# A selective-scan loop: the last 256 positions of a product moved to DMA and GpSimd, the other 768 formed one step ahead

## The chip, the cores and the metric

The kernel runs on one NeuronCore of a Trainium2 chip. The metric is the device time of one launch in microseconds. Below, PE is TensorE, DVE is VectorE, ACT is ScalarE, POOL is GpSimd, and SP is SyncE, which here issues the transfers.

## What is computed

Six residual layers on an image batch of 4 x 16 x 16 positions with 192 channels. The change touches the first alone, a state-space layer: after a projection, a 3x3 convolution and SiLU, four directions k are scanned over each image's 256 positions, for 96 channels with 16 states each, in float32:

```
def step(h, inp):
    u_t, d_t, B_t, C_t = inp
    dA = jnp.exp(d_t[..., None] * As)
    h = h * dA + (d_t * u_t)[..., None] * B_t[:, :, None, :]
    y = jnp.einsum('bkcn,bkn->bkc', h, C_t)
    return (h, y)
```

d is a softplus of a projection of the input; B and C are projections of it; u is the convolved input. The four directions are the image by rows, by columns, and both reversed. Their outputs are summed, normalised, gated by SiLU(z) and projected back to 192 channels. The other five layers (neighbourhood attention, a quantised transformer block, two expert layers and an attention) follow one after the other.

## The kernel before

All work is written out for each engine by hand, with semaphores between engines. The first layer is the function scan_layer. The 4 images of 256 positions lie side by side, so a row has T = 1024 columns. The 96 channels are cut into NG = 12 groups of 8, and a step puts 8 channels times 16 states on the 128 partitions. There are N = 48 steps (4 directions by 12 groups).

Ahead of the loop, ACT and DVE form d (tile dd) and d*u (tile du) for each direction on 96 partitions, and PE and ACT form B and C on 128 partitions (Bb, Cb). SP stores d in memory (scan_d, L438) and fetches it back for each step with each channel repeated for its 16 states (d_sp, L447), into NSP = 4 buffers.

Step n of the loop has these parts, each on its engine:

- ACT (L601): dA(n) = exp(A * d_sp) into PSUM banks 0-1 or 2-3. It waits until the scan of step n-2 has read that place.
- PE, spread(n) (L654): two matmuls with a 0/1 matrix (sel) copy the 8 rows of d*u to 128 partitions, in PSUM banks 4 and 5. Each half waits until the product of step n-1 has read it. A float32 matmul is recorded as two pieces.
- DVE (L502): two products dBu = (spread d*u) * Bb of 512 columns each, into one of two buffers.
- DVE (L509): the scan h = h * dA + dBu over 1024 columns into hs, one of two buffers. The sign of the step makes the reversed directions. It waits for both products of its step, for dA and for the product hC of step n-2.
- POOL (L470): hC = hs * Cb over 1024 columns, one of two buffers. For the last step DVE does it (L516).
- PE, add(n) (L669): two matmuls with selT sum the states of each channel and add the result in PSUM banks 6 and 7, which hold the sum y over steps.

PE's order is fixed by its own program, and each step n issues spread(n) and then add(n-2):

```
for n in range(N + 2):
    if n < N:
        spread(n)
    ...
    if n >= 2:
        add(n - 2)
```

Between spread(0) and spread(1) stands direct() (L659), two matmuls that need the last part of Cb. After the loop DVE, PE and ACT sum the directions, normalise, gate and project (L520 to L545).

Beside this, ACT quantises five weights for a later layer in some of the steps (L585), from a buffer that SP fills (L461).

Of the kernel before, what the change touches and what calls it, by code (L numbers as in the profile page):

```python
# [14 lines left out]
F32 = mybir.dt.float32  # L15
# [5 lines left out]
ALU = mybir.AluOpType  # L21
# [6 lines left out]
L = HW * HW  # L28
T = NB * L
C = 192  # L30
P = 128
CH = C // 2
NT = T // P
BANK = 512
NHALF = T // BANK
# [59 lines left out]
class GroupNorm:  # L95


    N = 2 * NB

# [97 lines left out]
DI = C // 2  # L197
NS = 16
RK = C // 16
CG = P // NS  # L200
NG = DI // CG
KD = 4
# [5 lines left out]
ORDER = (0, 2, 1, 3)  # L208
NSP = 4
# [4 lines left out]
def scan_layer(nc, const, X, D):  # L214
# [3 lines left out]
    with ExitStack() as stack:  # L218
        ctx = Ctx(nc, stack)
# [11 lines left out]
        sel = ctx.sb("sel", [DI, NG, P])  # L231
# [6 lines left out]
        zb = ctx.sb("zb", [DI, T])  # L238
        ps = ctx.ps("ps_l1", [P, 8, BANK])
        d_dram = nc.dram_tensor("scan_d", (KD, DI, T), F32, kind="Internal").ap()  # L240
        S = lambda n: ctx.sem(f"l1_{n}")
        loaded_xT = [S(f"loaded_xT{h}") for h in range(2)]
        loaded_g, loaded_w, loaded_p, loaded_s = S("loaded_g"), S("loaded_w"), S("loaded_p"), S("loaded_s")
# [6 lines left out]
        ordered, raw, bc_ps, bc_sb = S("ordered"), S("raw"), S("bc_ps"), S("bc_sb")  # L250
        soft_act, soft_vec, logged, d_ready, du_ready, A_done = (
            S("soft_act"), S("soft_vec"), S("logged"), S("d_ready"), S("du_ready"), S("A_done"))
        stored = [S(f"stored{k}") for k in range(KD)]
        spread_d = [S(f"spread_d{j}") for j in range(NSP)]
        started, dA_done, du_bc, dBu_done, scanned, weighted, y_added, y_out, weighted_last = (
            S("started"), S("dA_done"), S("du_bc"), S("dBu_done"), S("scanned"), S("weighted"), S("y_added"), S("y_out"),
            S("weighted_last"))
# [2 lines left out]
            S("turned"), S("stats"), S("var"), S("std"), S("rstd"), S("normed"), S("back"), S("gate"), S("res_ps"), S("res"))  # L260
        STEPS = 2 * NG
        N = 2 * STEPS
        banks = lambda a, b, rows=P: ps[0:rows, a:b, :].rearrange("p a b -> p (a b)")
        images = lambda a: a.rearrange("p (b h w) -> p b h w", h=HW, w=HW)
        turned_images = lambda a: a.rearrange("p (b w h) -> p b h w", h=HW, w=HW)
# [25 lines left out]
        with nc.Block() as block:  # L291
            @block.sync
            def _(sp_):
                for h in range(2):
                    sp_.dma_start(xT[:, h, :], D["xT"][:, h, :]).then_inc(loaded_xT[h], 16)
                sp_.dma_start(group[:, :], D["group"]).then_inc(loaded_g, 16)
                for dst, src in ((w_in, "w_in"), (cw, "cw"), (cb, "cb"), (const["ident"], "ident"), (Dk, "Dk"), (gamma, "out_g"),
                                 (beta, "out_b")):
                    sp_.dma_start(dst[:], D[src]).then_inc(loaded_w, 16)
                for dst, src in ((wdt, "wdt"), (dtw, "dtw"), (dtb, "dtb"), (Alog, "Alog")):  # L300
                    sp_.dma_start(dst[:], D[src]).then_inc(loaded_p, 16)
                sp_.dma_start(qw["sc"][:], D["q_scales"].partition_broadcast(P)).then_inc(q_loaded, 16)
                for dst, src in ((wB, "wB"), (wC, "wC"), (before, "before"), (sel, "sel"), (selT, "selT"), (w_out, "w_out0")):
                    sp_.dma_start(dst[:], D[src]).then_inc(loaded_s, 16)
                sp_.dma_start(X[:, :, :], D["x"].rearrange("(t p) c -> p t c", p=P)).then_inc(loaded_s, 16)
                sp_.wait_ge(zeroed, 1)
                sp_.dma_start(const["scratch_x"][:, 0:XW].rearrange("(p n) c -> p n c", p=P),
                              const["zero"][:, :].unsqueeze(1).broadcast_to([P, SLOTS // P, XW])).then_inc(const["scratch_clear"], 16)
                sp_.dma_start(const["scratch_g"][:, 0:XW].rearrange("(p n) c -> p n c", p=P),
                              const["zero"][:, :].unsqueeze(1).broadcast_to([P, G_BLOCKS, XW])).then_inc(const["scratch_clear"], 16)  # L310
                sp_.dma_start(const["scratch_g"][:, XW:XW + 4], D["g_spare"][0:G_BLOCKS * P, :]).then_inc(const["scratch_clear"], 16)
                sp_.dma_start(const["scratch_x"][:, XW:XW + 4], D["g_spare"]).then_inc(const["scratch_clear"], 16)
# [93 lines left out]
        Bb = ctx.sb("Bb", [P, KD, T])  # L406
# [3 lines left out]
        dd = ctx.sb("dd", [DI, KD, T])  # L410
        du = ctx.sb("du", [DI, KD, T])
        d_sp = ctx.sb("d_sp", [P, NSP, T])
        dBu = ctx.sb("dBu", [P, 2, T])
        hs = ctx.sb("hs", [P, 2, T])
        hC = ctx.sb("hC", [P, 2, T])
        ysum = ctx.sb("ysum", [DI, 2, T])
# [7 lines left out]
        dA = lambda n: banks(2 * (n % 2), 2 * (n % 2) + 2)  # L424
        which = lambda n: ORDER[n // NG]
# [7 lines left out]
        with nc.Block() as block:  # L433
            @block.sync
            def _(sync):
                def store(i):
                    sync.wait_ge(d_ready, i + 1)
                    sync.dma_start(d_dram[ORDER[i]], dd[:, i, :]).then_inc(stored[i], 16)  # L438

                def spread(n):  # L440
                    g = n % NG
                    if g == 0:
                        sync.wait_ge(stored[n // NG], 16)
                    if n >= NSP:
                        sync.wait_ge(dA_done, n - NSP + 1)
                    rows = d_dram[which(n), g * CG:(g + 1) * CG, :]
                    sync.dma_start(d_sp[:, n % NSP, :], rows.unsqueeze(0).broadcast_to([NS, CG, T])).then_inc(spread_d[n % NSP], 16)  # L447

                store(0)
                for n in range(NSP):  # L450
                    spread(n)
                for i in range(1, KD):
                    store(i)
                for n in range(NSP, N):
                    w = (n - Q_FIRST) // Q_EACH
                    if (n - Q_FIRST) % Q_EACH == 0 and w < len(q_weights):
                        if w == 0:
                            sync.wait_ge(soft_vec, 3 * KD)
                        else:
                            sync.wait_ge(qw["quantised"], 4 * w)  # L460
                        sync.dma_start(staged(w)[:, :], D[q_weights[w][0]]).then_inc(q_loaded, 16)  # L461
                    spread(n)

            @block.gpsimd
            def _(pool):
                for n in range(N - 1):
                    pool.wait_ge(scanned, n + 1)
                    if n >= 2:
                        pool.wait_ge(y_added, n - 1)
                    pool.tensor_tensor(hC[:, n % 2, :], hs[:, n % 2, :], Cb[:, which(n), :], ALU.mult).then_inc(weighted, 1)  # L470

            @block.vector
            def _(v):
# [18 lines left out]
                for i, k in enumerate(ORDER):  # L492
# [1 line left out]
                    v.tensor_tensor(dd[:, i, :], dd[:, i, :], du[:, i, :], ALU.add).then_inc(d_ready, 1)  # L494
                    v.wait_ge(d_ready, i + 1)
                    v.tensor_tensor(du[:, i, :], dd[:, i, :], xc[:, k % 2, :], ALU.mult).then_inc(du_ready, 1)
                for n in range(N):
                    if n % NG == 0:
                        v.wait_ge(bc_sb, 2 * (n // NG) + 1)
                    for half in range(NHALF):  # L500
                        v.wait_ge(du_bc, NHALF * n + half + 1)
                        v.tensor_tensor(dBu[:, n % 2, half * BANK:(half + 1) * BANK], ps[:, 4 + half, :],  # L502
                                        Bb[:, which(n), half * BANK:(half + 1) * BANK], ALU.mult).then_inc(dBu_done, 1)
                    v.wait_ge(dBu_done, NHALF * (n + 1))
                    v.wait_ge(dA_done, n + 1)
                    if n >= 2:
                        v.wait_ge(weighted, n - 1)
                    step = 1 if forward(n) else -1
                    v.tensor_tensor_scan(hs[:, n % 2, ::step], dA(n)[:, ::step], dBu[:, n % 2, ::step], 0.0,  # L509
                                         ALU.mult, ALU.add).then_inc(scanned, 1)  # L510
                n = N - 1
                v.wait_ge(scanned, N)
                v.wait_ge(y_added, N - 2)
                for half in range(NHALF):
                    at = slice(half * BANK, (half + 1) * BANK)
                    v.tensor_tensor(hC[:, n % 2, at], hs[:, n % 2, at], Cb[:, which(n), at], ALU.mult).then_inc(weighted_last, 1)  # L516
                for half in range(NHALF):
                    v.wait_ge(y_added, N + half)
                    at = slice(half * BANK, (half + 1) * BANK)
# [94 lines left out]
            def _(pe):  # L614
# [8 lines left out]
                for i, k in enumerate(ORDER):  # L623
# [4 lines left out]
                    for half in range(NHALF):  # L628
                        mm = pe.matmul(ps[0:DI, 2 * (i % 2) + half, :], W[:, k, :], xc[:, k % 2, half * BANK:(half + 1) * BANK],
                                       start=True, stop=True)  # L630
# [15 lines left out]
                def spread(n):  # L646
                    if n == 0:
                        pe.wait_ge(bc_sb, 2 * KD - 1)
                    if n % NG == 0:
                        pe.wait_ge(du_ready, n // NG + 1)  # L650
                    for half in range(NHALF):
                        if n >= 1:
                            pe.wait_ge(dBu_done, NHALF * (n - 1) + half + 1)
                        pe.matmul(ps[:, 4 + half, :], sel[:, n % NG, :], du[:, n // NG, half * BANK:(half + 1) * BANK],  # L654
                                  start=True, stop=True).then_inc(du_bc, 1)

                def direct():
                    for half in range(NHALF):
# [2858 lines left out]
```

## Time and profile before

| what | value |
|---|---|
| unprofiled runs, median of 3 | 1072.03 us (1070.88 to 1072.23) |
| span of the profiled execution, first to last instruction | 1079.8 us |
| busy PE / DVE / ACT / POOL over the span | 899.3 / 806.9 / 580.8 / 491.7 us |
| mean granted TensorE clock, 1 being 2.4 GHz | 0.845 |
| first scan starts, last scan starts | 81.59 us, 246.29 us |
| moved by DMA | 120.19 MB, 111 GB/s over the span |

The profiled execution's time without its profile is not among those shown; its span stands 7.8 us above the median of the other runs. Busy is the time in which an engine worked on an instruction; for PE the ends are modelled. The granted clock is that which the chip allowed TensorE; it has two levels, 2.4 GHz (1.00) and 1.2 GHz (0.50), and a figure between is a mean over a stretch. Steps of the loop are counted from 0.

### The profile page before, as it was taken

The page shows a single profiled execution, that of the slowest core. Times are in us where ns is not written, and L with a number is a line of the kernel's source. Part 1 is how long each engine was busy: PE and PEld are TensorE (multiplying, and loading weights), DVE is VectorE, ACT ScalarE, POOL GpSimd, SP SyncE. Part 2 cuts the span into 40 slices and gives each one's busy share as a digit, 9 for nine tenths or more (in the row PEclk, how much of TensorE's full clock was granted, in tenths as well). Part 3 has the DMA queues.
Part 4 walks back from the last instruction along what each step waited for, and adds up shares of the span by engine and source line. Part 5 has one row for each costly group of instructions (what it writes and reads, how often), then busy time and mean ns, then how long its engine had stood idle before and what let it go on. Part 6 is the DMA issues. An engine that isn't in the chain of part 4 may idle for free. (4 is left out here: it accounts for less than half of the span.)

```text
span 1079.8 us, 17931 instructions
## 1 busy us (share of the span) xinstructions
PE 899.3 (83%) x6186; PEld 592.0 (55%) x6186; DVE 806.9 (75%) x1719; ACT 580.8 (54%) x983; POOL 491.7 (46%) x499
## 2 busy tenths in 40 slices
PE   7469999996889977676778868899999978757985
PEld 3223333333459942233336337798888845557884
DVE  6279999997575458999996688578888676484665
ACT  2375445431357735676775454677666337255652
POOL 0006666664116607785872003367777500023873
PEclk9689999999799976555555569999999989978998
DMA  8648676532100000000000056589997276202454
GB/s 246 142 102 215 159 177 170 151 98 66 22 1 2 2 12 0 1 1 1 0 1 2 0 147 159 150 254 264 258 270 218 83 212 176 56 27 78 171 206 154
DMA packets 73019, 120.19 MB, mean 111 GB/s; under 512 B 24705, under 2 KB 47633, under 8 KB 72929
## 3 DMA queue, kind: packets, MB, share of 16 engines
q1 hardware_dynamic: 68080, 108.85, 36.9%
q0 software_dynamic: 4848, 10.20, 2.7%
q8 instruction: 50, 0.82, 0.3%
q14 instruction: 41, 0.33, 0.1%
HBM read 90.83 MB, written 19.40 MB: 102 GB/s over the span
## 5 line engine op out<-in xcount | busy, mean ns | idle before, releaser
L470 POOL TENSOR_TENSOR hC<-hs,Cb 128x1024 f32<-128x1024 f32 x47 | 110.8, 2358 | 134.2 <-DVE hs L509 134.2
L509 DVE TENSOR_TENSOR_SCAN hs<-ps_l,dBu 128x1024 f32<-128x1024 f32 x48 | 110.0, 2291 | 2.8 <-ACT ps_l L601 1.2
L669 PE MATMUL ps_l<-hC,selT 128*96 128x512 f32 x192 | 93.3, 609 | 1.5 <-POOL hC L470 1.5
L601 ACT ACTIVATE ps_l<-d_sp,Am 128x1020 f32<-128x1020 f32 x48 | 53.5, 1115 | 71.5 <-DVE hs L509 71.3
L654 PE MATMUL ps_l<-du,sel 96*128 96x512 f32 x192 | 90.5, 593 | 1.4 <-DVE dBu L502 1.4
L2176 POOL DMA_INDIRECT scratch_y<-m_o,m_xg x42 | 69.0, 1643 | 9.6 <-issue 9.6
L793 POOL TENSOR_TENSOR n_Pl<-n_PT,n_Ph 128x352 f16<-128x352 f32 x48 | 40.8, 852 | 66.1 <-ACT n_Ph L921 48.6
L2239 DVE TENSOR_TENSOR m_h_lo<-m_h,m_h_hi 128x512 f16<-128x512 f32 x62 | 42.8, 692 | 35.2 <-POOL m_h_hi L2153 32.2
L1772 PE MATMUL ps_l<-q_xi,identh 128*128 128x512 f16 x48 | 28.6, 595 | 48.0 <-POOL q_qi L1266 24.9
L2569 PE MATMUL ps_m<-m_wd_hi,m_h_hi 128*128 128x192 f16 x248 | 62.3, 251 | 5.4 <-DVE m_h_lo L2239 3.2
L2153 POOL CAST m_h_hi<-m_h 128x512 f16<-128x512 f32 x50 | 40.6, 813 | 57.5 <-DVE m_h L2228 57.4
L2815 POOL DMA_INDIRECT scratch_g<-g_U,g_slot x16 | 18.4, 1149 | 99.4 <-DVE g_who L2940 92.9
L502 DVE TENSOR_TENSOR dBu<-ps_l,Bb 128x512 f32<-128x512 f32 x96 | 60.7, 673 | 3.5 <-PE ps_l L654 3.4
L2571 PE MATMUL ps_m<-m_wd_hi,m_h_lo 128*128 128x192 f16 x248 | 62.5, 252 | 0.0
L654 PEld LDWEIGHTS ps_l<-du,sel 96*128 96x128 f32 x192 | 34.3, 188 | 51.1 <-DVE dBu L502 36.9
L2570 PE MATMUL ps_m<-m_wd_lo,m_h_hi 128*128 128x192 f16 x248 | 62.4, 251 | 0.0
L2455 ACT ACTIVATE m_act<-ps_m 128x512 f32<-128x512 f32 x62 | 36.8, 593 | 45.9 <-PE ps_m L2551 45.1
L669 PEld LDWEIGHTS ps_l<-hC,selT 128*96 128x96 f32 x192 | 27.4, 162 | 58.8 <-POOL hC L470 31.9
L2873 DVE TENSOR_TENSOR g_h_lo<-g_act,g_h_hi 128x384 f16<-128x384 f32 x46 | 26.6, 586 | 40.8 <-POOL g_h_hi L2843 23.6
L2165 POOL DMA_INDIRECT scratch_x<-m_U,m_slot x16 | 17.3, 1084 | 84.3 <-DMA m_U<-in_g_rows 75.1
L2547 PE MATMUL ps_m<-m_xt,m_wa_hi 128*128 128x256 f16 x184 | 50.3, 273 | 4.4 <-issue 3.2
L1626 ACT ACTIVATE q_pi<-q_ex,q_kf,q_fac 128x256 f16<-128x256 f32 x96 | 51.4, 590 | 0.8 <-PE ps_l L1764 0.8
(595 smaller groups left out, 3008.4 us busy)
## 6 DMA issues: line engine op xcount, KB each, us to landing
d_sp<-scan_d SPq DMA_DIRECT2D x48, 512.0 KB
m_sta<-in_m_ua SPq DMA_DIRECT2D x25, 512.0 KB
m_stb<-in_m_ub SPq DMA_DIRECT2D x50, 256.0 KB
m_std<-in_m_dn SPq DMA_DIRECT2D x25, 384.0 KB
gw_dn_in<-gw_dn SPq DMA_DIRECT2D x10, 576.0 KB
scratch_x<-zero SPq DMA_DIRECT2D x1, 4416.0 KB, 22.7
m_xg<-scratch_x SPq DMA_DIRECT2D x21, 193.0 KB, 5.9
gw_dn_in<-in_g_dn SPq DMA_DIRECT2D x5, 576.0 KB, 9.4
```

The source lines that it names most:

```text
L470: pool.tensor_tensor(hC[:, n % 2, :], hs[:, n % 2, :], Cb[:, which(n), :], ALU.mult).then_inc(weighted, 1)
L502: v.tensor_tensor(dBu[:, n % 2, half * BANK:(half + 1) * BANK], ps[:, 4 + half, :], Bb[:, which(n), half * BANK:(half + 1) * BANK], ALU.mu ...
L509: v.tensor_tensor_scan(hs[:, n % 2, ::step], dA(n)[:, ::step], dBu[:, n % 2, ::step], 0.0, ALU.mult, ALU.add).then_inc(scanned, 1)
L601: act.activation(dst[:, :, o:o + L - 1], d_sp[:, n % NSP, :].rearrange("p (b t) -> p b t", t=L)[:, :, o:o + L - 1], ACT.Exp, scale=Am[:, c ...
L654: pe.matmul(ps[:, 4 + half, :], sel[:, n % NG, :], du[:, n // NG, half * BANK:(half + 1) * BANK], start=True, stop=True).then_inc(du_bc, 1)
L669: mm = pe.matmul(ps[0:DI, 6 + half, :], selT[:, n % NG, :], hC[:, n % 2, half * BANK:(half + 1) * BANK], start=(n == STEPS), stop=(m == ST ...
L1626: act.activation(pi[:, p % 2, q, :], ex[:, p % NH, q, :], ACT.Identity, scale=fac[:, p % NH, q:q + 1], bias=kf[:, K_FLOOR:K_FLOOR + 1]).th ...
L2176: pool.indirect_dma_start(out=K["scratch_y"][:, :], out_offset=bass.IndirectOffsetOnAxis(ap=row.bitcast(U32), axis=0), in_=o_sb[:, n % M_O ...
L2547: pe.matmul(out, wa_hi[a][:, col], x[:, 0, :], start=True, stop=False)
L2569: pe.matmul(out, h_hi[:, b % 2, f // 2, tok], wd_hi[a][:, col], start=(f == 0), stop=False)
L2570: pe.matmul(out, h_hi[:, b % 2, f // 2, tok], wd_lo[a][:, col], start=False, stop=False)
L2571: mm = pe.matmul(out, h_lo[:, b % 2, f // 2, tok], wd_hi[a][:, col], start=False, stop=(f == tiles - 1))
```

## The change

Four things are changed in scan_layer, all for dBu, the product of d*u and B.

1. The last L = 256 columns of d*u (the fourth image) no longer go through PE. SP stores them in memory (scan_du, 96 x 256 for each direction) and fetches them for each step onto 128 partitions (du_sp, 4 buffers, 128 KB), behind the step's d_sp. POOL multiplies them with Bb. This is part(n); POOL issues part(n+1) ahead of hC(n).
2. PE's spread(n) makes 768 columns, by one matmul of 512 and one of 256, with a single signal after the second. It waits for the whole product of step n-1.
3. DVE multiplies the 768 columns in one operation, wide(n). It issues wide(0) ahead of the loop and then wide(n+1) ahead of scan(n). dBu has three buffers instead of two, and wide(n) and part(n) wait until scan(n-3) has read theirs.
4. The scan waits for wide(n) and for part(n).

The rest, PE's order of spread and add among it, is as it was.

```diff
--- before.py
+++ after.py
@@ -238,6 +238,7 @@
         zb = ctx.sb("zb", [DI, T])
         ps = ctx.ps("ps_l1", [P, 8, BANK])
         d_dram = nc.dram_tensor("scan_d", (KD, DI, T), F32, kind="Internal").ap()
+        du_dram = nc.dram_tensor("scan_du", (KD, DI, L), F32, kind="Internal").ap()
         S = lambda n: ctx.sem(f"l1_{n}")
         loaded_xT = [S(f"loaded_xT{h}") for h in range(2)]
         loaded_g, loaded_w, loaded_p, loaded_s = S("loaded_g"), S("loaded_w"), S("loaded_p"), S("loaded_s")
@@ -251,7 +252,10 @@
         soft_act, soft_vec, logged, d_ready, du_ready, A_done = (
             S("soft_act"), S("soft_vec"), S("logged"), S("d_ready"), S("du_ready"), S("A_done"))
         stored = [S(f"stored{k}") for k in range(KD)]
+        stored_du = [S(f"stored_du{k}") for k in range(KD)]
         spread_d = [S(f"spread_d{j}") for j in range(NSP)]
+        spread_du = [S(f"spread_du{j}") for j in range(NSP)]
+        dBu_part = S("dBu_part")
         started, dA_done, du_bc, dBu_done, scanned, weighted, y_added, y_out, weighted_last = (
             S("started"), S("dA_done"), S("du_bc"), S("dBu_done"), S("scanned"), S("weighted"), S("y_added"), S("y_out"),
             S("weighted_last"))
@@ -260,6 +264,7 @@
             S("turned"), S("stats"), S("var"), S("std"), S("rstd"), S("normed"), S("back"), S("gate"), S("res_ps"), S("res"))
         STEPS = 2 * NG
         N = 2 * STEPS
+        WIDE = T - L
         banks = lambda a, b, rows=P: ps[0:rows, a:b, :].rearrange("p a b -> p (a b)")
         images = lambda a: a.rearrange("p (b h w) -> p b h w", h=HW, w=HW)
         turned_images = lambda a: a.rearrange("p (b w h) -> p b h w", h=HW, w=HW)
@@ -410,7 +415,8 @@
         dd = ctx.sb("dd", [DI, KD, T])
         du = ctx.sb("du", [DI, KD, T])
         d_sp = ctx.sb("d_sp", [P, NSP, T])
-        dBu = ctx.sb("dBu", [P, 2, T])
+        du_sp = ctx.sb("du_sp", [P, NSP, L])
+        dBu = ctx.sb("dBu", [P, 3, T])
         hs = ctx.sb("hs", [P, 2, T])
         hC = ctx.sb("hC", [P, 2, T])
         ysum = ctx.sb("ysum", [DI, 2, T])
@@ -437,6 +443,10 @@
                     sync.wait_ge(d_ready, i + 1)
                     sync.dma_start(d_dram[ORDER[i]], dd[:, i, :]).then_inc(stored[i], 16)
 
+                def store_du(i):
+                    sync.wait_ge(du_ready, i + 1)
+                    sync.dma_start(du_dram[ORDER[i]], du[:, i, WIDE:T]).then_inc(stored_du[i], 16)
+
                 def spread(n):
                     g = n % NG
                     if g == 0:
@@ -445,12 +455,20 @@
                         sync.wait_ge(dA_done, n - NSP + 1)
                     rows = d_dram[which(n), g * CG:(g + 1) * CG, :]
                     sync.dma_start(d_sp[:, n % NSP, :], rows.unsqueeze(0).broadcast_to([NS, CG, T])).then_inc(spread_d[n % NSP], 16)
+                    if g == 0:
+                        sync.wait_ge(stored_du[n // NG], 16)
+                    if n >= NSP:
+                        sync.wait_ge(dBu_part, n - NSP + 1)
+                    rows = du_dram[which(n), g * CG:(g + 1) * CG, :]
+                    sync.dma_start(du_sp[:, n % NSP, :], rows.unsqueeze(0).broadcast_to([NS, CG, L])).then_inc(spread_du[n % NSP], 16)
 
                 store(0)
+                store_du(0)
                 for n in range(NSP):
                     spread(n)
                 for i in range(1, KD):
                     store(i)
+                    store_du(i)
                 for n in range(NSP, N):
                     w = (n - Q_FIRST) // Q_EACH
                     if (n - Q_FIRST) % Q_EACH == 0 and w < len(q_weights):
@@ -463,7 +481,17 @@
 
             @block.gpsimd
             def _(pool):
+                def part(n):
+                    if n % NG == 0:
+                        pool.wait_ge(bc_sb, 2 * (n // NG) + 1)
+                    pool.wait_ge(spread_du[n % NSP], 16 * (n // NSP + 1))
+                    if n >= 3:
+                        pool.wait_ge(scanned, n - 2)
+                    pool.tensor_tensor(dBu[:, n % 3, WIDE:T], du_sp[:, n % NSP, :], Bb[:, which(n), WIDE:T], ALU.mult).then_inc(dBu_part, 1)
+
+                part(0)
                 for n in range(N - 1):
+                    part(n + 1)
                     pool.wait_ge(scanned, n + 1)
                     if n >= 2:
                         pool.wait_ge(y_added, n - 1)
@@ -494,19 +522,25 @@
                     v.tensor_tensor(dd[:, i, :], dd[:, i, :], du[:, i, :], ALU.add).then_inc(d_ready, 1)
                     v.wait_ge(d_ready, i + 1)
                     v.tensor_tensor(du[:, i, :], dd[:, i, :], xc[:, k % 2, :], ALU.mult).then_inc(du_ready, 1)
-                for n in range(N):
+                def wide(n):
                     if n % NG == 0:
                         v.wait_ge(bc_sb, 2 * (n // NG) + 1)
-                    for half in range(NHALF):
-                        v.wait_ge(du_bc, NHALF * n + half + 1)
-                        v.tensor_tensor(dBu[:, n % 2, half * BANK:(half + 1) * BANK], ps[:, 4 + half, :],
-                                        Bb[:, which(n), half * BANK:(half + 1) * BANK], ALU.mult).then_inc(dBu_done, 1)
-                    v.wait_ge(dBu_done, NHALF * (n + 1))
+                    v.wait_ge(du_bc, n + 1)
+                    if n >= 3:
+                        v.wait_ge(scanned, n - 2)
+                    v.tensor_tensor(dBu[:, n % 3, 0:WIDE], banks(4, 6)[:, 0:WIDE], Bb[:, which(n), 0:WIDE], ALU.mult).then_inc(dBu_done, 1)
+
+                wide(0)
+                for n in range(N):
+                    if n + 1 < N:
+                        wide(n + 1)
+                    v.wait_ge(dBu_done, n + 1)
+                    v.wait_ge(dBu_part, n + 1)
                     v.wait_ge(dA_done, n + 1)
                     if n >= 2:
                         v.wait_ge(weighted, n - 1)
                     step = 1 if forward(n) else -1
-                    v.tensor_tensor_scan(hs[:, n % 2, ::step], dA(n)[:, ::step], dBu[:, n % 2, ::step], 0.0,
+                    v.tensor_tensor_scan(hs[:, n % 2, ::step], dA(n)[:, ::step], dBu[:, n % 3, ::step], 0.0,
                                          ALU.mult, ALU.add).then_inc(scanned, 1)
                 n = N - 1
                 v.wait_ge(scanned, N)
@@ -648,11 +682,11 @@
                         pe.wait_ge(bc_sb, 2 * KD - 1)
                     if n % NG == 0:
                         pe.wait_ge(du_ready, n // NG + 1)
-                    for half in range(NHALF):
-                        if n >= 1:
-                            pe.wait_ge(dBu_done, NHALF * (n - 1) + half + 1)
-                        pe.matmul(ps[:, 4 + half, :], sel[:, n % NG, :], du[:, n // NG, half * BANK:(half + 1) * BANK],
-                                  start=True, stop=True).then_inc(du_bc, 1)
+                    if n >= 1:
+                        pe.wait_ge(dBu_done, n)
+                    for at, end in ((0, BANK), (BANK, WIDE)):
+                        mm = pe.matmul(banks(4, 6)[:, at:end], sel[:, n % NG, :], du[:, n // NG, at:end], start=True, stop=True)
+                    mm.then_inc(du_bc, 1)
 
                 def direct():
                     for half in range(NHALF):
```

On PE, the loop's start. ps_l is PSUM, du and sel make the spread, diag and xc are direct(), hC and selT are the add. Before:

```order
L654 MATMUL ps_l<-du,sel 128x512 [waits l1_du_ready,l1_bc_sb]
L654 MATMUL ps_l<-du,sel 128x512
L659 MATMUL ps_l<-xc,diag 96x512 [waits l1_bc_sb]
L659 MATMUL ps_l<-xc,diag 96x512
L654 MATMUL ps_l<-du,sel 128x512 [waits l1_dBu_done] x4
L669 MATMUL ps_l<-hC,selT 96x512 [waits l1_weighted]
L669 MATMUL ps_l<-hC,selT 96x512
L654 MATMUL ps_l<-du,sel 128x512 [waits l1_dBu_done] x2
L669 MATMUL ps_l<-hC,selT 96x512 [waits l1_weighted]
L669 MATMUL ps_l<-hC,selT 96x512
```

and now:

```order
L688 MATMUL ps_l<-du,sel 128x512 [waits l1_du_ready,l1_bc_sb]
L688 MATMUL ps_l<-du,sel 128x256
L693 MATMUL ps_l<-xc,diag 96x512 [waits l1_bc_sb]
L693 MATMUL ps_l<-xc,diag 96x512
L688 MATMUL ps_l<-du,sel 128x512 [waits l1_dBu_done]
L688 MATMUL ps_l<-du,sel 128x256
L688 MATMUL ps_l<-du,sel 128x512 [waits l1_dBu_done]
L688 MATMUL ps_l<-du,sel 128x256
L703 MATMUL ps_l<-hC,selT 96x512 [waits l1_weighted]
L703 MATMUL ps_l<-hC,selT 96x512
L688 MATMUL ps_l<-du,sel 128x512 [waits l1_dBu_done]
L688 MATMUL ps_l<-du,sel 128x256
```

What moved: the second matmul of a spread has 256 columns in place of 512 and no wait of its own, and the order of spreads and adds is the same: spread(0), direct, spread(1), spread(2), add(0), spread(3).

On DVE, the loop's start. dBu<-ps_l,Bb is the product, and hs<-ps_l,dBu, named SCALAR_TENSOR_TENSOR here, is the scan. Before:

```order
L502 TENSOR_TENSOR dBu<-ps_l,Bb 128x512 [waits l1_du_bc,l1_bc_sb]
L502 TENSOR_TENSOR dBu<-ps_l,Bb 128x512 [waits l1_du_bc]
L509 SCALAR_TENSOR_TENSOR hs<-ps_l,dBu 128x1024 [waits l1_dA_done,l1_dBu_done]
L502 TENSOR_TENSOR dBu<-ps_l,Bb 128x512 [waits l1_du_bc] x2
L509 SCALAR_TENSOR_TENSOR hs<-ps_l,dBu 128x1024 [waits l1_dA_done,l1_dBu_done]
L502 TENSOR_TENSOR dBu<-ps_l,Bb 128x512 [waits l1_du_bc] x2
L509 SCALAR_TENSOR_TENSOR hs<-ps_l,dBu 128x1024 [waits l1_weighted,l1_dA_done,l1_dBu_done]
```

and now:

```order
L531 TENSOR_TENSOR dBu<-ps_l,Bb 128x768 [waits l1_du_bc,l1_bc_sb]
L531 TENSOR_TENSOR dBu<-ps_l,Bb 128x768 [waits l1_du_bc]
L543 SCALAR_TENSOR_TENSOR hs<-ps_l,dBu 128x1024 [waits l1_dA_done,l1_dBu_part,l1_dBu_done]
L531 TENSOR_TENSOR dBu<-ps_l,Bb 128x768 [waits l1_du_bc]
L543 SCALAR_TENSOR_TENSOR hs<-ps_l,dBu 128x1024 [waits l1_dA_done,l1_dBu_part,l1_dBu_done]
L531 TENSOR_TENSOR dBu<-ps_l,Bb 128x768 [waits l1_scanned,l1_du_bc]
L543 SCALAR_TENSOR_TENSOR hs<-ps_l,dBu 128x1024 [waits l1_dA_done,l1_weighted,l1_dBu_part,l1_dBu_done]
```

What moved: the product is one row of 768 columns, and there are two of them ahead of the first scan, so that each scan has the product of the step after it just ahead of it.

## Rows read from the trace of the kernel before

**Rows 1.** The page's costliest groups: line engine op, forms, count | busy us, mean ns | idle.
```profile
L470 POOL TENSOR_TENSOR hC<-hs,Cb 128x1024 f32<-128x1024 f32 x47 | 110.8, 2358 | 134.2 <-DVE hs L509 134.2
...
L502 DVE TENSOR_TENSOR dBu<-ps_l,Bb 128x512 f32<-128x512 f32 x96 | 60.7, 673 | 3.5 <-PE ps_l L654 3.4
```

**Rows 2.** Busy us (and count) of each engine from the first to the last scan.
```profile
core 0: us, PE busy (x) PEld busy (x) DVE busy (x) ACT busy (x) POOL busy (x), PEclk, DMA share, GB/s
81.60:246.30 164.70, 162.98 (x372) 59.45 (x370) 163.07 (x142) 77.31 (x76) 109.62 (x47) 1.00 0.60 157
```

**Rows 3.** The waits of DVE, 80 to 250 us: us in total, times, longest.
```profile
DVE hs L509 <- ACT ps_l L601: 1.2, 1, 1.2
```

**Rows 4.** Timeline of a step: start us, duration us, engine, line, what [idle before].
```profile
148.17 2.29 DVE L509 TENSOR_TENSOR_SCAN hs<-ps_l,dBu 128x1024 f32<-128x1024 f32 x1
...
150.38 1.26 DVE L502 TENSOR_TENSOR dBu<-ps_l,Bb 128x512 f32<-128x512 f32 x2
...
150.54 2.37 POOL L470 TENSOR_TENSOR hC<-hs,Cb 128x1024 f32<-128x1024 f32 x1 [1.15 <-DVE hs L509]
...
151.67 2.29 DVE L509 TENSOR_TENSOR_SCAN hs<-ps_l,dBu 128x1024 f32<-128x1024 f32 x1
```

**Rows 5.** Timeline of the loop's start.
```profile
77.77 1.88 PE L654 MATMUL ps_l<-du,sel 96*128 96x512 f32 x4
...
78.90 1.48 DVE L502 TENSOR_TENSOR dBu<-ps_l,Bb 128x512 f32<-128x512 f32 x2 [3.43 <-PE ps_l L654]
...
79.48 1.88 PE L659 MATMUL ps_l<-xc,diag 96*96 96x512 f32 x4
...
81.20 1.88 PE L654 MATMUL ps_l<-du,sel 96*128 96x512 f32 x4
...
81.59 2.29 DVE L509 TENSOR_TENSOR_SCAN hs<-ps_l,dBu 128x1024 f32<-128x1024 f32 x1 [1.21 <-ACT ps_l L601]
...
84.52 1.98 PE L654 MATMUL ps_l<-du,sel 96*128 96x512 f32 x4 [1.44 <-DVE dBu L502]
```

**Rows 6.** Timeline of the loop's end.
```profile
245.15 2.35 POOL L470 TENSOR_TENSOR hC<-hs,Cb 128x1024 f32<-128x1024 f32 x1 [1.15 <-DVE hs L509]
...
246.29 2.29 DVE L509 TENSOR_TENSOR_SCAN hs<-ps_l,dBu 128x1024 f32<-128x1024 f32 x1
...
247.56 1.96 PE L669 MATMUL ps_l<-hC,selT 128*96 128x512 f32 x4 [1.54 <-POOL hC L470]
```

**Rows 7.** Groups by form, 100 to 265 us: a 384-column product from PSUM.
```profile
L544 DVE TENSOR_TENSOR X<-X,ps_l 128x384 f32<-128x384 f32 x4 | 2.2, 553 | 0.7 <-PE ps_l L696 0.4
```

**Rows 8.** Windows of stretches at either clock, columns as in rows 2.
```profile
66.00:73.00 7.00, 4.28 (x5) 1.85 (x6) 6.90 (x7) 4.03 (x5) 0.00 (x0) 0.50 0.42 119
84.00:88.00 4.00, 3.48 (x8) 1.25 (x8) 3.96 (x5) 1.61 (x2) 2.85 (x2) 1.00 1.03 246
250.00:264.00 14.00, 10.50 (x68) 8.37 (x66) 9.43 (x34) 2.12 (x5) 2.60 (x1) 1.00 0.09 25
410.80:414.20 3.40, 1.10 (x8) 0.22 (x4) 1.43 (x4) 2.16 (x4) 2.27 (x6) 1.00 0.00 0
414.20:418.00 3.80, 2.45 (x7) 0.59 (x8) 3.08 (x7) 2.48 (x4) 3.38 (x5) 0.51 0.00 0
660.00:663.40 3.40, 3.40 (x24) 3.08 (x22) 2.70 (x9) 1.11 (x2) 2.22 (x2) 0.50 1.00 297
663.40:666.80 3.40, 3.40 (x33) 3.05 (x32) 3.17 (x12) 1.23 (x2) 0.88 (x1) 0.99 0.53 166
```

**Rows 9.** Timeline of PE, 411 to 415 us, in the quantised layer.
```profile
411.89 0.39 PE L1752 MATMUL ps_l<-q_qkb 16*128 16x256 bf16 x2 [0.37 <-ACT q_lt L1617]
414.99 0.61 PE L1772 MATMUL ps_l<-q_xi,identh 128*128 128x512 f16 x1 [2.71 <-POOL q_qi L1266]
```

## The prediction

> **What bounds the kernel now.** I read four views in this order: the costliest groups, the windows of the scan loop, the waits of DVE in it, and the timeline of a step. The groups [rows 1] show that the loop's work on DVE is, beside 48 scans of 2.29 us [rows 4], 96 half products of 673 ns, and on POOL 47 products of 2358 ns. From the first scan (starts at 81.59, [rows 5]) to the last (starts at 246.29, [rows 6]) are 164.70 us, or 3.504 us for each of 47 steps. In that stretch [rows 2] DVE is busy 163.07 us and PE 162.98, both 99%, at a granted clock of 1.00, and POOL 109.62 us (67%). DVE's only wait is one of 1.2 us at the start [rows 3]. The reader is to see in the timeline [rows 4] that DVE sets the pace: scan at 148.17, two half products at 150.38, scan again at 151.67. That is 2.21 us from scan to product and 1.29 us from product to scan. PE needs 1.72 us for each of its two jobs (79.48 to 81.20 in [rows 5]), 3.44 of 3.50 us. PE is nearly the bound as well, and its order is fixed by the program: spread(n), add(n-2), spread(n+1).
>
> **The change on DVE: shorter.** Names are those of the order above: wide(n) is the 768-column product, part(n) the 256-column one on POOL. A 384-column product from PSUM takes 553 ns [rows 7] and one of 512 takes 673 [rows 1], 0.94 ns a column, so 768 columns take about 0.91 us. A half product and its follower overlap by 0.08 us (pair 1.26 us against 2 x 0.67), which leaves 0.86 (rounded up) from wide to scan. DVE alone would then need 2.21 + 0.86 = 3.07 us a step.
>
> **PE: shorter.** Four recorded pieces of 512 columns take 1.72 us, 0.43 each. The spread becomes two of 512 and two of 256: 0.86 + 0.43 = 1.29 us. With add that is 3.01 us a step.
>
> **POOL: longer, hidden.** part is not in the trace. Below, a quarter of 2.36 us is 0.59; above, a whole one, 2.36. It is a tensor product of the same two kinds of operand as hC, so I take 0.6: 2.96 us a step. It would be on the path if DVE ran at 3.07, and is not at the pace found below. Even 2.36 + 2.36 = 4.7 us would only just reach it.
>
> **SP and DMA: hidden.** Each step adds an issue and 128 KB to 512 KB. Before, the loop's queue moved 157 GB/s at a DMA share of 0.60 [rows 2], so 640 KB in the 4.5 us or more found below is about 145 GB/s, less than now, and the issues (one now takes some 0.5 us) are two in 4.5 us. The landing has about four steps before it is needed. The cover goes only if the step shrinks to 3.1 us (some 210 GB/s, still under the 246 of [rows 8]).
>
> **The wait that the change adds.** DVE runs strictly in program order, and wide(n+1) now stands ahead of scan(n). wide(n+1) waits for spread(n+1) on PE. There spread(n+1) still stands behind add(n-2), which waits for POOL's hC(n-2), which waits for scan(n-2). So the scan of two steps earlier must go through POOL, PE twice and DVE before scan(n) may start: a loop of waits over two steps. Before, it was spread(n+1) ahead of dBu(n+1), one step later on DVE, and it had room: hC ends 0.05 us before its add starts and spread is over before it is wanted. Its length now, from the end of one scan to the end of the scan two later:
> - to hC's start 0.08 (scan ends at 150.46, hC starts 150.54, [rows 4]); hC 2.36; to add 0.06 (247.50 to 247.56, [rows 6])
> - add 1.72, spread 1.29, its drain 0.16 (1.88 against 1.72), and 0.10 for weights loaded by an idle PE (1.98 against 1.88, [rows 5])
> - to wide 0.11 (the first half is out at 77.77 + 0.86 + 0.16, the product starts at 78.90, [rows 5])
> - wide 0.86, scan 2.29.
>
> The sum is 9.03 us for two steps, 4.5 a step where it is 3.5 now. The other scan of each pair has its own such loop. Nothing spreads the two evenly: scan(0) and scan(1) can start 3.1 us apart, because add stands ahead only from spread(3) on, so pairs stay bunched: gaps of 3.1 and 5.9 us. Then the loop has 23 pairs and one short step: 23 x 9.03 + 3.1 = 210.8 us, 46.1 more than 164.7.
>
> **Start.** spread(1) follows direct() on PE and wide(1) follows spread(1). spread(0) from 77.77 takes 1.29, direct 1.72, spread(1) 1.29 + 0.16, to wide 0.1, wide 0.86: scan(0) starts at 83.2 instead of 81.59, 1.6 us later. The du part must first be stored and spread back; the second of them lands behind 1.8 MB (two times 640 KB and the two stores), 7.3 us at the 246 GB/s of [rows 8], so by 76 from a start at 68.5; at half that rate by 83.3, just in time. I take it as hidden. Clearing nine more semaphores, and the end of the layer: nothing, beside other work.
>
> **The clock.** Each pair keeps PE busy for about 6 us and then leaves it idle from 8.6 to 11.5 us after the scan's end, 2.9 us. The trace has such a gap: PE idle 2.71 us [rows 9], 1.10 us busy in the stretch around it, and the clock was at its half level (1.2 GHz; granted 0.51) right after [rows 8]. A gap of 1.44 us [rows 5] left it at 1.00 [rows 8]. So I expect it to fall in most pairs and to come back once PE has been dense: in one place after a stretch of 3.40 us with PE busy throughout, in another after 4.28 us of matmuls [rows 8], with full speed of the pieces from 77.77 on [rows 5]. PE does half its work in such a stretch, so a fall costs 1.7 to 2.1 us of the loop of waits. With a fall in about five of six pairs (my choice: one gap in the trace is no proof for all) that is 1.6 us a pair: 23 x 1.6 = 37 us. The bounds are 0 (no fall) and 3.0 (always at half: PE itself needs 4 x 3.01 = 12.0 us a pair).
>
> [...]
>
> **Sum.** 46.1 + 1.6 + 37 = 84.7, less about 1 for the last pair, whose add leads to no scan: +83. The profiled execution spans 1079.8 us; the median of the three unprofiled runs is 1072.03 and no unprofiled time of the profiled execution is shown, so I take the difference to hold for both: span 1163, **time 1155 us**.
>
> **Rivals.**
> 1. The loop of waits closes, but the clock holds. For it: mean PE load is 6 of 9 us, and 14 us behind the loop with PE busy 10.50 keep the full clock [rows 8]. Against it: there the load came without one long gap, and the gap of [rows 9] is as long as these. Time: 1072 + 46.1 + 1.6 = 1120.
> 2. PE stays at half clock nearly throughout: 23 x 12.0 + 3.1 = 279.1, 114.4 more, 1188. Against it: a PE that is always busy got its clock back in both places of [rows 8].
> 3. The other side: the loop of waits does not bind and DVE's shorter work does. It decides if hC, add and spread of one step fit into DVE's work of two steps, that is if 9.03 were under 2 x 3.07 = 6.14; or if spread(n+1) could be had before add(n-2). Then 47 x 3.07 = 144.3, 20.4 less, 1.6 more at the start: 1053. For it: DVE, PE and POOL all have under 3.1 us of work a step. Against it: the order, and each duration is from its own row.
> 4. The edit isn't what it says: forming one step ahead would bring nothing if the scan still had to wait for its own product; but it waits for one formed a step earlier. What is true in this is that ahead on DVE without ahead on PE is the wait above.
>
> **How the numbers follow.** The forecast gets 0.68 (1135 to 1170), rival 1 gets 0.18 (1112 to 1125, with its latencies 0.15 us a pair either way), falls in only some pairs between them 0.05, rival 2 gets 0.05, rival 3 gets 0.03, the remainder 0.01 near no change. The range 1112 to 1170 leaves out about one in ten beside the tails of the forecast itself. A measurement of this kernel can tell 0.2%, 2.1 us. Faster 0.03, same 0.01, slower 0.96.
>
> **What would show it.** DVE busy in the loop falls from 99% to about two thirds; the 768-column product shows an idle before it that ends with PE's spread, about 2.8 us in every second step and none in the other; add is released by hC with PE idle before; the granted clock in the loop is about 0.8 instead of 1.00. Wrong would be: even steps of 3.1 us (the loop of waits does not close), a clock of 1.00 (rival 1), waits of the scan for part or of part for its DMA (POOL or DMA mispriced).

## The result, and the profile after

The changed kernel takes 1162.26 us (median of 4 runs, 1158.12 to 1166.60) against 1072.11 us before (4 runs, 1070.88 to 1072.23): 1.083 times as long, 95% interval 1.080 to 1.087. That is 90 us more, inside the range of 1112 to 1170 and 7 us above the predicted 1155. Of the ten runs of the last experiment below one (1087.76 us) is slow, over 1.5% above the fastest, and is left out of its ratio.

The costliest groups of the changed kernel's page that belong to the loop; columns as in [rows 1]:

```profile
L703 PE MATMUL ps_l<-hC,selT 128*96 128x512 f32 x192 | 125.7, 792 | 65.7 <-POOL hC L498 65.7
L498 POOL TENSOR_TENSOR hC<-hs,Cb 128x1024 f32<-128x1024 f32 x47 | 110.4, 2349 | 115.6 <-DVE hs L543 115.3
...
L531 DVE TENSOR_TENSOR dBu<-ps_l,Bb 128x768 f32<-128x768 f32 x48 | 45.4, 946 | 111.5 <-PE ps_l L688 111.5
L543 DVE TENSOR_TENSOR_SCAN hs<-ps_l,dBu 128x1024 f32<-128x1024 f32 x48 | 109.3, 2279 | 0.0
...
L490 POOL TENSOR_TENSOR dBu<-du_sp,Bb 128x256 f32<-128x256 f32 x48 | 34.8, 726 | 76.0 <-DMA du_sp<-scan_du 76.0
```

The scan still takes 2.28 us and POOL's product still 2.35. The one DVE product of 768 columns takes 946 ns, and POOL's part 726. What is new are the idle times: DVE sat idle for 111.5 us ahead of wide, each time until PE's spread (L688) was done, and PE for 65.7 us ahead of add, each time until POOL's hC was done. POOL's 76.0 us ahead of part stand almost all ahead of the loop, before the first part at 76.5 us; the other 2.0 end at 79.31, ahead of the first scan as well.

The window from the first scan to the last of the changed kernel, 85.1 to 335 us:

```profile
core 0: us, PE busy (x) PEld busy (x) DVE busy (x) ACT busy (x) POOL busy (x), PEclk, DMA share, GB/s
85.10:335.00 249.90, 186.59 (x368) 77.54 (x368) 144.83 (x95) 76.29 (x75) 139.44 (x92) 0.82 0.51 127
```

The loop takes 249.9 us where it took 164.70 [rows 2]. DVE's busy share fell from 99% to 58%, PE's from 99% to 75%, and the clock from 1.00 to 0.82. DVE's waits from 80 to 340 us (engine, line, who ended them, us in total, times, longest) are a single group, where [rows 3] had 1.2 us:

```profile
DVE dBu L531 <- PE ps_l L688: 111.5, 25, 5.8
```

Two of these waits, 6.5 us together, stand ahead of the first scan. The other 23, 105.0 us, are one in each pair of steps.

One pair of steps of the changed kernel, from scan(4) to scan(6), from its timeline:

```profile
107.56 2.28 DVE L543 TENSOR_TENSOR_SCAN hs<-ps_l,dBu 128x1024 f32<-128x1024 f32 x1
...
109.76 0.93 DVE L531 TENSOR_TENSOR dBu<-ps_l,Bb 128x768 f32<-128x768 f32 x1
...
109.92 2.35 POOL L498 TENSOR_TENSOR hC<-hs,Cb 128x1024 f32<-128x1024 f32 x1 [4.53 <-DVE hs L543]
110.61 2.28 DVE L543 TENSOR_TENSOR_SCAN hs<-ps_l,dBu 128x1024 f32<-128x1024 f32 x1
...
112.33 3.20 PE L703 MATMUL ps_l<-hC,selT 128*96 128x512 f32 x4 [2.67 <-POOL hC L498]
...
115.32 1.96 PE L688 MATMUL ps_l<-du,sel 96*128 96x512 f32 x4
...
117.31 0.96 DVE L531 TENSOR_TENSOR dBu<-ps_l,Bb 128x768 f32<-128x768 f32 x1 [4.42 <-PE ps_l L688]
...
118.18 2.28 DVE L543 TENSOR_TENSOR_SCAN hs<-ps_l,dBu 128x1024 f32<-128x1024 f32 x1
```

Here the loop of waits can be read off. Scan(4) ends at 109.84. hC(4) starts at 109.92 and ends at 112.27. Then add(4) starts at 112.33, at half clock, and behind it on PE spread(7) at 115.32. wide(7) has waited 4.42 us for it and starts at 117.31, and scan(6), which stands behind wide(7) on DVE, starts at 118.18. From the end of scan(4) to that of scan(6), 120.46, are 10.62 us. The scans are 3.05 us apart (107.56, 110.61) and then 7.57 us (118.18).

The clock over the same pair and the start of the next, in windows of the changed kernel:

```profile
112.30:115.70 3.40, 3.37 (x5) 1.41 (x6) 0.59 (x1) 2.80 (x3) 3.39 (x3) 0.59 0.99 217
115.70:119.00 3.30, 3.30 (x9) 1.47 (x8) 1.69 (x2) 0.00 (x0) 0.30 (x1) 0.91 0.68 174
119.00:122.40 3.40, 1.28 (x4) 0.40 (x3) 3.40 (x3) 1.90 (x2) 1.86 (x1) 1.00 0.00 0
122.40:125.90 3.50, 2.96 (x4) 1.15 (x5) 1.11 (x1) 1.82 (x2) 3.49 (x4) 0.61 0.83 202
```

The clock is at half for most of 112.3 to 115.7, right behind the 2.67 us in which PE stood idle. It is back at full by 119, holds over the stretch in which PE is busy 1.28 of 3.40 us, and is down again behind it.

### The profile page after: what moved, and what is told of

It reads as the page before. It is cut to its first block and busy times, and to the rows that moved or that the text cites. A ratio compares the mean times of both kernels' runs of the same rounds, so it can differ in the third digit from the quotient of the medians.

```text
span 1162.1 us, 18129 instructions
## 1 busy us (share of the span) xinstructions
PE 919.2 (79%) x6186; PEld 611.8 (53%) x6186; DVE 789.1 (68%) x1671; ACT 580.2 (50%) x983; POOL 522.7 (45%) x547
## 5 line engine op out<-in xcount | busy, mean ns | idle before, releaser
L703 PE MATMUL ps_l<-hC,selT 128*96 128x512 f32 x192 | 125.7, 792 | 65.7 <-POOL hC L498 65.7
L531 DVE TENSOR_TENSOR dBu<-ps_l,Bb 128x768 f32<-128x768 f32 x48 | 45.4, 946 | 111.5 <-PE ps_l L688 111.5
L703 PEld LDWEIGHTS ps_l<-hC,selT 128*96 128x96 f32 x192 | 36.8, 204 | 116.0 <-POOL hC L498 72.7
L688 PE MATMUL ps_l<-du,sel 96*128 96x512 f32 x192 | 81.0, 549 | 1.1 <-DVE dBu L531 1.1
L688 PEld LDWEIGHTS ps_l<-du,sel 96*128 96x128 f32 x192 | 44.0, 230 | 65.0 <-issue 58.0
L490 POOL TENSOR_TENSOR dBu<-du_sp,Bb 128x256 f32<-128x256 f32 x48 | 34.8, 726 | 76.0 <-DMA du_sp<-scan_du 76.0
```

Source lines behind the costliest of these rows:

```text
L531: v.tensor_tensor(dBu[:, n % 3, 0:WIDE], banks(4, 6)[:, 0:WIDE], Bb[:, which(n), 0:WIDE], ALU.mult).then_inc(dBu_done, 1)
L688: mm = pe.matmul(banks(4, 6)[:, at:end], sel[:, n % NG, :], du[:, n // NG, at:end], start=True, stop=True)
L703: mm = pe.matmul(ps[0:DI, 6 + half, :], selT[:, n % NG, :], hC[:, n % 2, half * BANK:(half + 1) * BANK], start=(n == STEPS), stop=(m == ST ...
```

## The experiments

Six kernels were run, all of them edits of the changed kernel. The kernel before ran beside them, with medians of 1071.39 us (beside the first three and the fifth below) and 1073.16 (beside the fourth and the sixth). The names wide, part, spread and add are those of the change.

### PE one spread ahead as well

```diff
+                spread(0)
                 for n in range(N + 2):
-                    if n < N:
-                        spread(n)
                     if n == 0:
                         pe.wait_ge(bc_sb, 2 * KD)
                         direct()
+                    if n + 1 < N:
+                        spread(n + 1)
```

> The changed kernel with one more edit: PE issues spread(n+1) ahead of add(n-2), as DVE issues wide(n+1) ahead of scan(n). Theory (a loop of waits scan, hC, add, spread, wide, scan over two steps sets the pace): the loop is cut, DVE works without idle at 2.20 + 0.85 = 3.05 us a step, 47 steps take 143.4 us against 164.7 before and 250.0 with the change, the clock stays at 1.00 in it, and the time is 1053 us (1050 to 1058). Rival (the split itself costs: POOL's part, its DMA, or DVE and POOL in each other's way): PE's order does not matter, the time stays above 1140 us. A milder form of it: POOL at 2.31 + 0.72 = 3.03 us a step just binds, 3.1 to 3.3 us a step, 1056 to 1066 us.

Measured: 1054.23 us (4 runs, 1053.24 to 1054.79), 0.983 of before, interval 0.979 to 0.987. Windows of the loop's first steps, of the loop, and of its middle, columns as above, and one step and a half of its timeline:

```profile
83.90:87.30 3.40, 1.91 (x5) 0.82 (x6) 3.40 (x3) 1.12 (x1) 1.33 (x1) 1.00 1.08 390
87.30:90.70 3.40, 3.40 (x6) 1.53 (x5) 3.06 (x3) 1.11 (x1) 3.39 (x3) 0.50 1.06 239
92.00:226.00 134.00, 133.57 (x352) 58.25 (x350) 133.34 (x89) 73.07 (x72) 132.60 (x88) 1.00 0.92 221
110.00:215.00 105.00, 105.00 (x278) 45.69 (x277) 105.00 (x70) 55.17 (x57) 104.84 (x70) 1.00 0.97 232
```

```profile
120.69 2.36 POOL L498 TENSOR_TENSOR hC<-hs,Cb 128x1024 f32<-128x1024 f32 x1
...
121.38 2.28 DVE L543 TENSOR_TENSOR_SCAN hs<-ps_l,dBu 128x1024 f32<-128x1024 f32 x1
...
121.84 1.46 PE L688 MATMUL ps_l<-du,sel 96*128 96x512 f32 x4
...
123.01 0.72 POOL L490 TENSOR_TENSOR dBu<-du_sp,Bb 128x256 f32<-128x256 f32 x1
...
123.13 1.93 PE L703 MATMUL ps_l<-hC,selT 128*96 128x512 f32 x4
123.57 0.93 DVE L531 TENSOR_TENSOR dBu<-ps_l,Bb 128x768 f32<-128x768 f32 x1
...
123.73 2.36 POOL L498 TENSOR_TENSOR hC<-hs,Cb 128x1024 f32<-128x1024 f32 x1
...
124.42 2.28 DVE L543 TENSOR_TENSOR_SCAN hs<-ps_l,dBu 128x1024 f32<-128x1024 f32 x1
```

The scans stand at 121.38 and 124.42. No DVE row shown has an idle time, and from 92 to 226 us DVE waits once, for 0.7 us. The spread (121.84) now stands ahead of the add (123.13), and POOL goes from hC (120.69) to part (123.01) and at 123.73 to hC again, with next to no gap. Steps are 3.05 us but for two near the start (3.49 and 3.82), where the clock is at half from 87.3 to 90.7, and the last (2.42), and first to last scan takes 143.8 us. The split, its DMA and POOL's work are all still there, so none of them made the kernel slow by itself; DVE one step ahead of PE's order did. The theory stands and the strong rival falls. The mild one, that POOL binds, is not seen either, but POOL is busy 132.6 of 134 us.

The ring of waits is not gone here. By the program's order spread(n+1) now stands behind add(n-3), so the ring spans three steps; with the 8.93 us that the run with fillers measures below, that is 2.98 us a step against the 3.05 that DVE takes.

### The split without one step ahead

```diff
-                wide(0)
                 for n in range(N):
-                    if n + 1 < N:
-                        wide(n + 1)
+                    wide(n)
```

> The changed kernel with wide(n) right ahead of scan(n) on DVE, so one step ahead is undone and the split to DMA and POOL kept. Theory: the same chain of 9 us now spans three steps, 3.0 us each, and no longer binds; DVE sets 2.20 + 0.93 = 3.13 us a step, 47 steps 147 us, the time is 1056 us (1053 to 1062), clock 1.00 in the loop. Rival (the split costs): 1140 us or more, as now.

Measured: 1057.35 us (4 runs, 1056.16 to 1058.32), 0.986 of before, interval 0.982 to 0.990. Its loop:

```profile
84.00:232.00 148.00, 145.48 (x367) 60.73 (x368) 146.41 (x94) 76.49 (x76) 140.28 (x93) 1.00 0.90 219
```

Every step takes 3.17 us, 0.04 more than expected, and from the first scan on DVE waits for nothing; a wait of 1.3 us for dA stands just ahead of that scan. So of the change's two ideas the split (with the single product and the third buffer, which this run keeps) is worth 14 us by itself, and one step ahead, put on it alone, costs 105 us; with PE's order changed too it is worth another 3 us.

### The clock held up by fillers

```diff
                     mm.then_inc(du_bc, 1)
+                    if n >= 2 and n % 2 == 0 and n != STEPS + 2:
+                        for f in range(12):
+                            pe.matmul(ps[0:DI, 6 + f % 2, 0:XW], const["zero"][:, 0:DI], const["zero"][:, :], start=False, stop=False)
```

> The changed kernel with 12 matmuls of zeros (384 columns, float16, added to the sums in PSUM banks 6 and 7, so that nothing changes in them) after each spread of an even step from 2 on, except step 26, where PE is idle for about 2.7 us. It takes the clock's part away and leaves the loop of waits. Theory: the clock is 1.00 in the loop, pairs take 9.0 us, the loop 23 x 9.0 + 3.1 = 210 us against 250.0, the time is 1120 us (1116 to 1128). Rival (the clock's falls cost nothing, since something else sets 10.6 us a pair): 1158 to 1170 us. If the fillers delay the next add, up to 1 us a pair more, 1140 us.

Measured: 1121.18 us (4 runs, 1120.10 to 1123.03), 1.046 of before, interval 1.041 to 1.050. Its loop, and a pair of steps:

```profile
88.00:292.00 204.00, 186.44 (x616) 91.98 (x616) 139.92 (x91) 75.18 (x74) 137.41 (x92) 0.99 0.59 149
```

```profile
101.18 2.28 DVE L543 TENSOR_TENSOR_SCAN hs<-ps_l,dBu 128x1024 f32<-128x1024 f32 x1
...
103.14 2.12 PE L692 MATMUL ps_l<-zero 128*96 128x384 f16 x12
...
103.54 2.36 POOL L498 TENSOR_TENSOR hC<-hs,Cb 128x1024 f32<-128x1024 f32 x1 [2.85 <-DVE hs L543]
104.22 2.28 DVE L543 TENSOR_TENSOR_SCAN hs<-ps_l,dBu 128x1024 f32<-128x1024 f32 x1
...
105.95 1.96 PE L706 MATMUL ps_l<-hC,selT 128*96 128x512 f32 x4 [0.69 <-POOL hC L498]
...
107.75 1.46 PE L688 MATMUL ps_l<-du,sel 96*128 96x512 f32 x4
...
109.24 0.96 DVE L531 TENSOR_TENSOR dBu<-ps_l,Bb 128x768 f32<-128x768 f32 x1 [2.74 <-PE ps_l L688]
...
110.11 2.28 DVE L543 TENSOR_TENSOR_SCAN hs<-ps_l,dBu 128x1024 f32<-128x1024 f32 x1
```

The fillers (L692) run from 103.14 to 105.26, in PE's gap, which shrinks to 0.69 us; add starts at 105.95, released by hC as before. The chain can be measured at full clock: scan ends 103.46, hC 103.54 to 105.90, add 105.95, spread 107.75 to 109.21, wide 109.24, scan 110.11 to 112.39. That is 8.93 us. Scans are 3.04 to 3.11 and 5.83 to 5.89 us apart, all but the one pair at step 26 that has no filler, and there the gap is 7.59 us. The loop takes 209.4 us. PE did more work, and the kernel became 41 us faster than the changed one: those 41 us were the clock's.

### Fewer fillers

The same edit with range(4) in place of range(12).

> The changed kernel with 4 matmuls of zeros in place of the 12 of the run with fillers, so that PE's idle gap of 2.7 us shrinks to about 2.0 us. Theory (the gap makes the clock fall, and only the fall costs beyond 8.9 us a pair): the falls become fewer or stay as they are, never more; the time lies between 1121 and 1162 us, likeliest 1145, with the mean granted clock in the loop between 0.81 and 0.98, and pairs of 8.9 us wherever the clock held. Rival (the fillers help in another way than by the clock, for example by keeping PE's queue awake): 1121 us at a clock that still falls.

Measured: 1149.05 us (4 runs, 1146.60 to 1150.66), 1.069 of before, interval 1.066 to 1.072.

```profile
88.00:280.00 192.00, 152.77 (x370) 67.10 (x370) 116.72 (x77) 65.34 (x64) 115.30 (x76) 0.88 0.61 148
```

PE's gap ahead of add is about 2.0 us now, where it was 2.67. The long gaps between scans are of two kinds and nothing between: 6 of 5.85 to 5.88 us, and 17 of 7.47 to 7.58 us. The record of the granted clock has 17 stretches at half in this loop, as many as there are long gaps, so a fall of the clock either happens in a pair or not, and one costs 1.7 us. The clock's mean is 0.88. The rival, that fillers help in another way than by the clock, would have given short gaps throughout at a clock that still falls. The time is 4 us above the likeliest value and inside the range.

### One step ahead without the split

All columns by PE and DVE: no scan_du, du_sp or part, and

```diff
-                    v.tensor_tensor(dBu[:, n % 3, 0:WIDE], banks(4, 6)[:, 0:WIDE], Bb[:, which(n), 0:WIDE], ALU.mult).then_inc(dBu_done, 1)
+                    v.tensor_tensor(dBu[:, n % 3, :], banks(4, 6), Bb[:, which(n), :], ALU.mult).then_inc(dBu_done, 1)
...
-                    for at, end in ((0, BANK), (BANK, WIDE)):
+                    for at, end in ((0, BANK), (BANK, T)):
```

> The changed kernel without the split: PE spreads and DVE multiplies all 1024 columns in one operation, no second DMA and no part on POOL; one step ahead and three buffers stay. Theory: the chain is 9.03 + 0.43 (spread) + 0.27 (wide) = 9.7 us a pair at the full clock, 226 us for the loop, 1135 us, and with falls of the clock as now (up to 2.1 us a pair) 1135 to 1185 us; the likeliest is 1165. Rival (the split costs, one step ahead does not): 1070 to 1080 us.

Measured: 1183.27 us (4 runs, 1182.04 to 1187.12), 1.104 of before, interval 1.099 to 1.109.

```profile
85.00:355.00 270.00, 210.64 (x368) 77.87 (x368) 159.16 (x94) 76.30 (x75) 108.07 (x46) 0.81 0.37 92
```

One step ahead is slow without any split: the loop takes 270.3 us, two pairs take 9.6 us and the others 11.1 to 12.7, at a mean clock of 0.81. It came near the upper end of what was expected.

### The same with PE one spread ahead

Both edits above together.

> All 1024 columns by PE and one DVE operation, one step ahead on DVE, and PE's spread(n+1) ahead of add(n-2): what one step ahead is worth alone once both engines are ahead. Theory: the loop of waits is cut, and PE's own work (four matmuls of 0.86 us, 3.44 us a step) is the bound before DVE's 2.20 + 1.12 = 3.32 us: 3.44 to 3.50 us a step, clock 1.00, time 1069 us (1066 to 1073). Rival (one step ahead costs in itself, for example by the third buffer or the longer product): 1080 us or more.

Measured: 1072.24 us (10 runs, 1069.83 to 1087.76), 0.999 of before, interval 0.997 to 1.001; it lies 3 us above the likeliest 1069, inside its range, and cannot be told from before.

```profile
100.00:220.00 120.00, 120.00 (x281) 48.91 (x280) 119.31 (x71) 61.53 (x62) 82.36 (x36) 1.00 0.67 166
```

PE is busy the whole window, at full clock, and a step takes 3.44 us, which is its 4 x 0.86 us of matmuls. The loop is 160.0 us, 4.7 less than before, but its first scan comes at 86.1, 4.5 us later, which takes it back. So one step ahead without the split is worth nothing here even when both engines are ahead: PE, the second bound all along with its 3.44 us, now sets the step.

## Why the prediction was right, and where its sizes were off

**The loop of waits.** Right. The predicted 9.03 us a pair is 8.93 at full clock. The term that differs most is the hand-over to wide, 0.03 us for 0.11; add with its start after the gap is 1.80 for 1.82. The pairs stay bunched, 3.05 us and the rest, as foretold. The ring over two steps is shown by undoing it in two ways (PE ahead, DVE not ahead), after which the long waits are gone, and by the waits' names. The idle time ahead of every second product was put at 2.8 us; it is 2.74 with fillers and 4.42 in the pair shown of the changed kernel, where the clock's fall stands in it.

**The clock.** Right in kind; this is the mis-sized term. I took a fall in five of six pairs at 1.6 us a pair on average, 37 us. In the changed kernel no pair took 8.9 us: every one lost something, the pairs being 10.3 to 12.0 us, with a median of 10.6. Over the 23 pairs, (249.9 - 2.2) / 23 = 10.77 us, 1.84 more than 8.93, which is 42 us; the runs with and without fillers differ by 41. The 2.2 is what stands between the last two scans, not the 3.1 that I had, because the last step has no wide behind it. Four pairs took 11.9 or 12.0, the 3.0 us of the upper bound. The two errors pull against each other: the ring is 0.10 us a pair too long in the prediction and the falls 5 us too small in all, so part of the closeness of the total is luck. The record of the granted clock has a stretch at half in each of the 23 pairs. The Trainium skill's page "TensorE: Matmul & The Clock Gate", section "HAM oscillation — how this bites in real kernels", tells of a kernel whose bursts of matmuls each start at the half clock, behind waits of about 3 to 5 us. The trace agrees that the fall comes in every burst, and shows it behind shorter waits, of 2.67 us.

**The sum.** The loop grew by 85.2 us in the profiled executions (82 was the sum's). Its start came 3.5 us later (1.6 predicted): 1.3 of that stood there already at ACT's four logarithms (63.86 before, 65.14 now), ahead of anything that the change edits. It need not come from the change: two of the edited kernels have the changed kernel's code up to there and start the logarithms at 63.95 and 65.80; why it moves is open. And one term was missing, the end. The last two adds, eight pieces, take 3.76 us before and 5.37 with the change, since the gap ahead of them, 3.95 us for 1.54, left the clock down. Before:

```profile
247.56 3.76 PE L669 MATMUL ps_l<-hC,selT 128*96 128x512 f32 x8 [1.54 <-POOL hC L470]
```

and now:

```profile
337.52 5.37 PE L703 MATMUL ps_l<-hC,selT 128*96 128x512 f32 x8 [3.95 <-POOL hC L498]
```

That is 1.6 us. Another 1.3 come ahead of it: from the last scan's start to these adds are 1.27 us before and 2.55 now, since the last two scans are 2.2 us apart instead of 3.5 and the adds still wait for the hC between them. I had put the end at nothing. Loop, start and end together give 91.6 us at the layer's end; the medians differ by 90 us. The spans differ by 82.3, because the profiled execution of before spent 833.5 us behind the loop and that of the change 827.1; six other kernels with the same code there took 822 to 828 us. I took the difference of spans and medians to be the same, and it was not: before's profiled execution was 7.8 us above its median, the change's 0.2 below.

**POOL and DMA.** Hidden, as said: from the first scan on POOL never waits for du_sp. part took 0.72 us, not 0.6: a quarter of the columns takes more than a quarter of the time. At 3.05 us a step this matters, since hC to part is 2.32 us and part 0.72, 3.04 in all.

**Rivals.** Rival 1 (chain alone, 1120) is the run with fillers, 1121. Rival 3 (1053) did not come here; its condition, that spread(n+1) could be had before add(n-2), is what the run with PE ahead makes true, and that run takes 1054. Rival 2 did not come: the clock came back in every pair, and its mean in the loop is 0.82.

## What to carry to other kernels

When a step is formed one ahead on one engine, walk the whole ring of engines: whatever that engine now waits for must also be one ahead on the engine that makes it, or the in-order queues close a loop over fewer steps than before. Add the durations round that loop and divide by the steps it spans; 8.9 us over three steps was free here, since DVE took 3.17 a step, and over two it was 4.5 where DVE needs 3.05. If a wait leaves PE idle for some microseconds in each round, price the clock too: here it added 41 us to a loss of 50.

## What the runs showed of the hardware that was not expected

Gaps of 2.65 to 3.07 us in PE, one in each of 23 pairs, brought the clock to half in every one (PE busy 186.59 of the loop's 249.90 us). Gaps cut to about 0.7 us by matmuls of zeros (1.11 in the first pair) did it in none; only the pair that was left without fillers, with a gap of 2.67 us, lost its clock. A PE with more to do made the kernel 41 us faster.

The length of the gap alone does not decide. With four fillers PE's gaps are 1.96 to 2.02 us in 21 of 23 pairs, and the clock fell in 16 of those and held in 5. A longer one, 2.42 us in the first pair, left it at full. In the run with PE ahead, gaps of 1.05 and 1.49 us ahead of 86.8 us were enough once, where the 1.44 us of [rows 5] were not.

The second transfer costs little more than its bytes. In the trace of the run with PE ahead, packets of 1 KB (du_sp) take 74 ns in the mean from first to last scan, and packets of 4 KB (d_sp) 264 ns. With 128 packets each, a du_sp takes 0.59 us of all 16 engines and a d_sp 2.12 us: for a quarter of the bytes 0.28 of the time, 1.12 times as much a byte. I had put the faster loop at some 210 GB/s and saw room up to 246; it moves 221 at a share of 0.92, and 232 at 0.97 in its middle. A still shorter step may find DMA as its bound; that was not tried.
